# Neighbour counts made once, beside the third layer's gathers, and read back by two sum rounds

## The chip, the core and the metric

The kernel runs on one core of a Trainium2 chip. Five engines take part: PE (TensorE) for matmuls, DVE (VectorE) and ACT (ScalarE) for elementwise work, POOL (GpSimd), which here issues the gathers, and SP, whose queue carries most other transfers. The metric is the device time of one execution in microseconds; smaller is better.

## What is computed

A stack of four graph layers over 6250 nodes of 128 features, on one list of 106,250 edges sorted by target node, each followed by a residual and a layer norm:

```python
x = _layernorm(x + _L0_gnn_ref(x, edge_type_16, ...))   # two relational convolutions, 16 relations
x = _layernorm(x + _L1_gnn_ref(x, ...))                 # attention, 8 heads
x = _layernorm(x + _L2_gnn_ref(x, edge_type_8, ...))    # relational, 8 relations: the "third layer" here
x = _layernorm(x + _L3_gnn_ref(x, ...))                 # two plain mean aggregations
# in L3, twice:
msg_sum = jax.ops.segment_sum(x[src], dst, num_segments=n)
deg = jax.ops.segment_sum(jnp.ones_like(dst, dtype=x.dtype), dst, num_segments=n)
return (msg_sum / jnp.maximum(deg, 1.0)[:, None]) @ W_l.T + b + x @ W_r.T
```

The change concerns the third layer and the two sums `msg_sum` of the fourth, called sum rounds here.

## The kernel before

The edges are cut into 832 tiles of 128, and these into 104 batches of 8. A gathered batch is eight indirect DMAs issued by POOL (`gather_near`, `gather_mixed`), each of which fetches 128 rows of 512 bytes by the indices that ACT has copied into `IDX`. Matmuls with one-hot matrices made by DVE then sum the rows by target node.

**The third layer** (`near_round` with `near_c`) goes through all 104 batches, four in an iteration, with four row buffers. For batch k, PE multiplies the sums of batch k-1 by eight relation matrices (L1320, "products"), then the gathered rows by one-hots (L1330, two units of four matmuls, "near matmuls"), then places batch k-1 (L1338). ACT copies each unit out of PSUM (L942, "near copy"), copies the product (L934), and stages the indices four batches ahead (L923). DVE makes the one-hots of the next batch (L1885) and adds a placed batch to the sums (L1969).

**The sum rounds** (`mixed_round`, for `mix_a` and `mix_b`) treat every third batch without a gather: a *dense* batch. For each of its 8 tiles DVE makes two one-hots (`hot`, L2326 and L2327), PE multiplies them into counts of (source node, target) pairs (`build`, L1543), and ACT writes these to one of two blocks `NEIGH` (`take_out`, L867). PE then multiplies 49 slices of the block with the node features, split into three bf16 parts (`apply`, L1550). That makes 34 dense and 70 gathered (*sparse*) batches per round. PE's order in a step: transpose a block for the ground (L1606), half of a dense batch's products with builds for the next one between them, the ground term (L1611, L1612), and the sparse batch's eight matmuls (`collect`, L1622). POOL has four row buffers and issues batch g+3 once `collect` of g-1 is done. Every engine's order is written out by hand, and semaphores join them.

## Time and profile before

| what | us |
|---|---|
| median of 3 runs (6337.29 to 6344.32) | 6337.98 |
| profiled execution | 6346.25 |
| its span, first to last instruction | 6344.3 |
| third layer's gathered round, 3741 to 4786 | 1045 |
| first sum round, from its first gather, 4841 to 5557 | 716 |
| second sum round, 5582 to 6298 | 716 |

Over the span PE is busy for 71%, POOL for 70%, DVE for 44% and ACT for 30%. Such shares are averages over stages with different limits, so each stage has to be read by itself. An engine's busy time leaves out the instructions that only issue, load registers or wait; "idle" is told with what ended it, and "issue" is a pause in which the engine waited for nothing that the profile shows.

### The profile page before, as it was taken

The page shows a single profiled execution, that of the slowest core. Times are in us where ns is not written, and L with a number is a line of the kernel's source. Part 1 is how long each engine was busy: PE and PEld are TensorE (multiplying, and loading weights), DVE is VectorE, ACT ScalarE, POOL GpSimd, SP SyncE. Part 2 cuts the span into 40 slices and gives each one's busy share as a digit, 9 for nine tenths or more (in the row PEclk, how much of TensorE's full clock was granted, in tenths as well). Part 3 has the DMA queues.
Part 4 walks back from the last instruction along what each step waited for, and adds up shares of the span by engine and source line. Part 5 has one row for each costly group of instructions (what it writes and reads, how often), then busy time and mean ns, then how long its engine had stood idle before and what let it go on. Part 6 is the DMA issues. An engine that isn't in the chain of part 4 may idle for free. (4 is left out here: it accounts for less than half of the span.)

```text
span 6344.3 us, 119904 instructions
## 1 busy us (share of the span) xinstructions
PE 4533.7 (71%) x27080; PEld 3709.3 (58%) x27081; DVE 2761.6 (44%) x10683; ACT 1904.5 (30%) x4793; POOL 4416.5 (70%) x4559
## 2 busy tenths in 40 slices
PE   3488887878778886566666675565555888778886
PEld 3377777767777775455555555555554555555554
DVE  6643333333333332566666542222225554355543
ACT  0022222222222223444444441111114333243332
POOL 3067777757777773777777647777775777767777
PEclk6599999999999997566666688878887999989998
DMA  3066666642222211333333322111121222222222
GB/s 79 3 168 161 156 154 156 158 119 53 53 53 53 53 52 44 89 83 83 83 83 83 71 63 52 52 52 52 52 52 52 54 53 54 53 63 54 54 53 59
DMA packets 380915, 478.11 MB, mean 75 GB/s; under 512 B 123697, under 2 KB 293202, under 8 KB 380242
## 3 DMA queue, kind: packets, MB, share of 16 engines
q0 software_dynamic: 142336, 295.20, 18.3%
q1 hardware_dynamic: 233778, 174.99, 10.9%
q14 instruction: 591, 4.84, 0.2%
q10 hardware_dynamic: 4128, 1.75, 0.1%
q8 instruction: 82, 1.34, 0.1%
HBM read 447.41 MB, written 24.15 MB: 74 GB/s over the span
## 5 line engine op out<-in xcount | busy, mean ns | idle before, releaser
L1320 PE MATMUL PS<-ROOM 128*128 128x128 f32 x8320 | 1028.4, 282 | 130.6 <-ACT ROOM L942 130.6
L1320 PEld LDWEIGHTS PS<-ROOM 128*128 128x128 f32 x8320 | 972.9, 195 | 200.5 <-ACT ROOM L942 147.7
L942 ACT COPY ROOM<-PS 128x512 f32<-128x512 f32 x1040 | 609.7, 586 | 1390.5 <-PE PS L1330 1387.1
L777 POOL DMA_INDIRECT GB<-table,IDX x832 | 793.0, 953 | 316.6 <-issue 252.1
L747 POOL DMA_INDIRECT GB<-table,IDX x576 | 571.4, 992 | 217.5 <-issue 174.4
L1969 DVE TENSOR_TENSOR ROOM<-ROOM,PS 128x128 f32 x312 | 89.7, 288 | 1362.7 <-PE PS L1338 1359.0
L777 POOL DMA_INDIRECT GB<-in_x,IDX x416 | 402.8, 968 | 370.7 <-ACT IDX L923 234.0
L747 POOL DMA_INDIRECT ROOM<-table,IDX x544 | 519.1, 954 | 165.8 <-issue 164.9
L1330 PE MATMUL PS<-OH,GB 128*128 128x256 f32 (+1 forms) x1664 | 387.9, 403 | 314.4 <-DMA GB<-table,IDX 253.0
L1330 PEld LDWEIGHTS PS<-OH,GB 128*128 128x128 f32 x1664 | 326.4, 248 | 361.3 <-issue 288.2
L735 POOL DMA_INDIRECT GB<-table_gat,IDX x416 | 426.6, 1025 | 127.7 <-issue 124.2
L735 POOL DMA_INDIRECT H<-table_gat,IDX x416 | 416.6, 1002 | 126.9 <-issue 121.4
L777 POOL DMA_INDIRECT H<-in_x,IDX x416 | 404.4, 972 | 126.8 <-issue 126.8
L777 POOL DMA_INDIRECT H<-table,IDX x416 | 397.3, 955 | 126.8 <-issue 124.1
L777 POOL DMA_INDIRECT ROOM<-table,IDX x416 | 396.4, 953 | 126.8 <-issue 124.1
L1463 PE MATMUL PS<-ROOM,OH 128*128 128x144 f32 x1664 | 431.9, 453 | 1.2 <-DVE ROOM L2120 1.2
L1463 PEld LDWEIGHTS PS<-ROOM,OH 128*128 128x128 f32 x1664 | 398.2, 332 | 2.8 <-issue 1.3
L1543 PE MATMUL PS<-SPARE 128*128 128x400 bf16 x1088 | 272.6, 344 | 164.0 <-DVE SPARE L2327 144.9
L1880 DVE SCALAR_TENSOR_TENSOR H<-iota_w,key,ROOM 128x256 f32<-128x256 f32 x416 | 173.9, 482 | 345.6 <-PE PS L1330 134.5
L1330 PE MATMUL PS<-OH,ROOM 128*128 128x128 f32 x832 | 171.7, 391 | 207.7 <-DMA ROOM<-table,IDX 207.7
L1550 PE MATMUL PS<-ROOM 128*128 128x384 bf16 x1666 | 311.5, 327 | 4.5 <-issue 2.5
L1550 PE MATMUL PS<-ROOM,PACK 128*128 128x384 bf16 x1666 | 310.2, 328 | 1.7 <-issue 0.3
(386 smaller groups left out, 8405.6 us busy)
## 6 DMA issues: line engine op xcount, KB each, us to landing
H<-one_over SPq DMA_DIRECT2D x416, 128.0 KB
ROOM<-one_over SPq DMA_DIRECT2D x416, 128.0 KB
ROOM<-local_row SPq DMA_DIRECT2D x104, 256.0 KB
GB<-table,IDX POOLq DMA_INDIRECT x1408
ROOM<-table,IDX POOLq DMA_INDIRECT x960
GB<-in_x,IDX POOLq DMA_INDIRECT x416
H<-in_x,IDX POOLq DMA_INDIRECT x416
H<-table,IDX POOLq DMA_INDIRECT x416
```

The source lines that it names most:

```text
L735: pool.indirect_dma_start(out=out[:, j, :], out_offset=None, in_=r.table.dram[:, :], in_offset=bass.IndirectOffsetOnAxis(ap=idx[:, j:j + 1 ...
L747: pool.indirect_dma_start(out=RING_ROWS[c][:, j * P:(j + 1) * P], out_offset=None, in_=m.table.dram[:, :], in_offset=bass.IndirectOffsetOn ...
L777: pool.indirect_dma_start(out=r.rows[c][:, j * P:(j + 1) * P], out_offset=None, in_=r.dram[:, :], in_offset=bass.IndirectOffsetOnAxis(ap=I ...
L942: act.copy(to.rearrange("p r (j d) -> p r j d", j=r.per), of.rearrange("p (j d r) -> p r j d", j=r.per, d=NEAR))\
L1320: ins = nc.tensor.matmul(PS[:, 4, 0:P], r.near[1 - b][:, t * P:(t + 1) * P], r.weights[:, t * P:(t + 1) * P], start=t == 0, stop=t == r.re ...
L1330: ins = nc.tensor.matmul(PS[:, n, j % r.per * r.cols:(j % r.per + 1) * r.cols], r.rows[c][:, j * P:(j + 1) * P], r.hot[b][:, j * r.cols:(j ...
L1463: ins = nc.tensor.matmul(PS[:, 1 - b, 0:MW_COLS], hot(1 - b)[:, j, :], MW[:, 1 - b, j, :], start=j == 0, stop=j == G - 1)
L1543: ins = nc.tensor.matmul(PS[:, 2 * b + a, 0:KEYS // 2], HOT_LO[b], HOT_KEY[b][:, a * KEYS // 2:(a + 1) * KEYS // 2], start=True, stop=True)
L1550: ins = nc.tensor.matmul(PS[:, 4 + e, 0:3 * P], NEIGH[e][:, h, :], XS[:, h, :], start=h == 0, stop=h == XBLOCKS - 1)
L1880: ins = dve.scalar_tensor_tensor(to, columns, key, WINDOWS[b][:, j * r.cols:(j + 1) * r.cols], ALU.is_equal, ALU.mult, accum_out=wstage[:, ...
L1969: dve.tensor_tensor(dst, dst, PS[:, 5, 0:P], ALU.add).then_inc(added, 1)
```

## The change

Every four batches now form a group: the first two (16 tiles) are dense, the last two sparse. That makes 26 dense steps and 52 sparse batches per sum round. The counts of all 26 x 16 tiles are made once, in the loop of the third layer: DVE makes the one-hots (`hot_tiles`, and adds up columns in `correct`), PE multiplies them (`count_tile`) into one pair of PSUM banks, ACT takes them out (`take_out`). A tile now has 12 columns, one per node, not 16, and is written at the node's own offset in a block for 128 targets; a column that a tile shares with the one before is kept aside and added by DVE. Each finished block (`MADE_UP`, one buffer) is stored to DRAM by SP (`neighbours`); both sum rounds load blocks into the two `NEIGH` buffers. No builds are left in the sum rounds, and the one-hots of a sparse batch are one instruction, not eight. A small table (`keyed` steps) says whether a group's 16 tiles span at most 128 nodes; if not, a slow path is taken.

The core of the diff:

```diff
-KEYS = NHI * NEAR
-DENSE = BATCHES // 3
-SPARSE = BATCHES - DENSE
+SPAN = 12
+KEYS = NHI * SPAN
+PAIR = 2 * G
+CYCLE = 4
+DENSE = BATCHES // CYCLE
+SPARSE = BATCHES - 2 * DENSE
+STRIDE = 136
...
+        TILES_OF = (range(0), range(0, 5), range(5, 10), range(10, 16))
...
# SP
+            with sp.Fori(0, DENSE) as d:
+                sp.wait_ge(mx_cor, d * PAIR + PAIR)
+                sp.dma_start(neighbours[bass.ds(d, 1), :, :].rearrange("o p s -> (o p) s"), MADE_UP).then_inc(made_out, 16)
+
+            def load(m, d, e):
+                if not isinstance(d, int) or m.d0 + d >= 2:
+                    sp.wait_ge(mx_app, d + (m.d0 - 1))
+                sp.dma_start(NEIGH[e].rearrange("p h s -> p (h s)"),
+                             neighbours[bass.ds(d, 1), :, :].rearrange("o p s -> (o p) s")).then_inc(mx_ld[e], 16)
...
# ACT, third layer
+            def take_out(d, n, j, offsets):
+
+                t = d * PAIR + j
+                if j == 0:
+                    if not isinstance(d, int) or d > 0:
+                        act.wait_ge(made_out, d * 16)
+                        act.sem_inc(near_passed, 1)
+                if n == 0 and (not isinstance(t, int) or t > 0):
+                    act.wait_ge(mx_cor, t)
+                    act.sem_inc(near_passed, 1)
+                if not isinstance(t, int) or t > 0:
+                    act.wait_ge(mx_out, t)
+                    act.sem_inc(near_passed, 1)
+                act.wait_ge(mx_built, t + 1)
+                act.sem_inc(near_passed, 1)
+                if j == 0:
+                    act.copy(MADE_HALVES[:, :, :, 0:SPAN], counted_of(2)).then_inc(mx_out, 1)
+                else:
+                    act.copy(MADE_HALVES[:, :, :, bass.ds(offsets[n] + 1, SPAN - 1)], counted_of(2)[:, :, :, 1:SPAN])
+                    act.copy(SIDE[:, n, :].rearrange("p (a h) -> p a h", a=2), counted_of(2)[:, :, :, 0]).then_inc(mx_out, 1)
...
# PE, third layer
+            def count_tile(d, n, j):
+
+                t = d * PAIR + j
+                pe.wait_ge(mx_hot, t + 1)
+                if not isinstance(t, int) or t > 0:
+                    pe.wait_ge(mx_out, t)
+                for a in range(2):
+                    ins = nc.tensor.matmul(PS[:, 2 + a, 0:KEYS // 2], HOT_LO[:, n, :], HOT_KEY[n][:, a * KEYS // 2:(a + 1) * KEYS // 2],
+                                           start=True, stop=True)
+                ins.then_inc(mx_built, 1)
...
+                    tiles = TILES_OF[c] if counting and now < BATCHES else range(0)
+                    if tiles:
+                        for n in range(2):
+                            count_tile(i, n, tiles[n])
...
+                            if tiles:
+                                for at in range(2 + 2 * n, 4 if n == 0 else len(tiles)):
+                                    count_tile(i, at, tiles[at])
...
# PE, sum rounds
+                    if half == 0:
+                        pe.wait_ge(mx_ld[e], i * 16 + 16 * (m.d0 // 2 + 1))
+                        pe.sem_inc(g_passed, 1)
                     for w in range(4 * half, 4 * half + 4):
-                        if not isinstance(d, int) or d < DENSE - 1:
-                            for j in tiles_of(w):
-                                build(d + 1, j)
...
# DVE, third layer
+            def hot_tiles(d, tiles, some):
+
+                n0 = d * (CYCLE * G) + tiles[0]
+                m = len(tiles)
+                if some[0] == 0:
+                    dve.tensor_tensor(HOT_LO[:, 0:m, :], mid(iota_h[:, 0:P], m), last(lo_col[:, bass.ds(n0, m)], P), ALU.is_equal)
+                for n in some:
+                    dve.tensor_scalar(HOT_KEY[n], iota_h[:, :], near_col[:, bass.ds(n0 + n, 1)], None, ALU.is_equal).then_inc(mx_hot, 1)
+
+            def correct(d, tiles, offsets):
+
+                for n, j in enumerate(tiles):
+                    if j == 0:
+                        dve.sem_inc(mx_cor, 1)
+                        continue
+                    dve.wait_ge(mx_cor, d * PAIR + j)
+                    column = MADE_HALVES[:, :, :, bass.ds(offsets[n], 1)].rearrange("p a h o -> p (a h) o")
+                    dve.tensor_tensor(column, column, SIDE[:, n, :].unsqueeze(2), ALU.add).then_inc(mx_cor, 1)
...
+                        if mine:
+                            offsets = offsets_of(dve, i, mine)
+                            dve.wait_ge(mx_out, i * PAIR + (mine[-1] + 1))
+                            dve.sem_inc(near_passed, 1)
+                        if later:
+                            hot_tiles(i, later, range(2))
+                        if mine:
+                            correct(i, mine, offsets)
+                        if later:
+                            hot_tiles(i, later, range(2, len(later)))
...
# DVE, sum rounds
-                    for j in range(part * G // 2, (part + 1) * G // 2):
-                        ins = dve.tensor_scalar(oh(b, j), iota_f[:, :], local[:, bass.ds(n + j, 1)], None, ALU.is_equal)
-                    if part == 1:
-                        ins.then_inc(mx_oh, 1)
+                    dve.tensor_tensor(OH[:, b, :].rearrange("p (j n) -> p j n", j=G), mid(iota_f[:, :], G),
+                                      last(local[:, bass.ds(n, G)], P), ALU.is_equal).then_inc(mx_oh, 1)
```

How the order of instructions moves is seen best in three places. First ACT's own stream in the loop of the third layer, one batch of four, before:

```order
L934 COPY same<-PS 128x128
L939 ISA
L942 COPY ROOM<-PS 128x8x64
L939 REGISTER_ALU
L942 COPY ROOM<-PS 128x8x64
L923 ISA
L923 COPY IDX<-idx 128x8
```

and now, the first part of the first counted batch (`meta` is the table of offsets, `128x50x12` and `128x50x11` a tile's counts, `SPARE` the column kept aside):

```order
L997 COPY same<-PS 128x128
L586 ISA
L586 TENSOR_LOAD meta
L586 ISA x10
L967 REGISTER_ALU
L975 REGISTER_ALU
L978 CAST ROOM<-PS 128x50x12
L975 REGISTER_ALU
L980 ISA
L980 COPY ROOM<-PS 128x50x11
L981 CAST SPARE<-PS 128x50
L1007 ISA
```

Between the copy of the product and the first near copy (L1010, after the last row) there now stand a table read and two take-outs; two more follow each near copy.

Second, PE in a sum round, the second half of a dense step, before:

```order
L1606 MATMUL PS<-ident,STG 128x128
L1543 MATMUL PS<-SPARE 128x400 x2
L1550 MATMUL PS<-ROOM 128x384 x6
L1543 MATMUL PS<-SPARE 128x400 x2
L1550 MATMUL PS<-ROOM 128x384 x6
L1611 MATMUL PS<-turned,STG 128x128
L1612 MATMUL PS<-bias_rows,ones_mat 128x128
L1543 MATMUL PS<-SPARE 128x400 x2
L1550 MATMUL PS<-ROOM 128x384 x13
```

and now:

```order
L1685 MATMUL PS<-ident,STG 128x128
L1630 MATMUL PS<-ROOM 128x384 x12
L1690 MATMUL PS<-turned,STG 128x128
L1691 MATMUL PS<-bias_rows,ones_mat 128x128
L1630 MATMUL PS<-ROOM 128x384 x13
L1696 COMPARE_AND_BRANCH
L1701 MATMUL PS<-OH,GB 128x128 x8
```

The builds (L1543) that waited for DVE and ACT are gone from between the products.

Third, SP's queue after the third layer has begun, where before only the stores of the node table stood:

```order
L744 UNCONDITIONAL_BRANCH
L744 ISA
L746 ISA
L746 DMA neighbours<-ROOM 128x6800
L744 REGISTER_ALU
L744 COMPARE_AND_BRANCH
L751 DMA ROOM<-neighbours 128x6800
L751 DMA PACK<-neighbours 128x6800
L742 DMA table<-X 128x4x128 x12
```

One store per group was put into a loop, and the first two loads stand ahead of the table's stores.

## Rows read from the trace of the kernel before

**Rows 1.** Busy time by engine in three stretches; last TensorE clock, DMA share, GB/s.

```profile
3741.00:4786.00 1045.00, 607.78 (x3532) 558.89 (x3532) 226.03 (x1032) 167.32 (x425) 791.62 (x832) 0.81 0.20 52
4841.00:5557.00 716.00, 589.05 (x3676) 391.85 (x3676) 351.10 (x1351) 258.68 (x461) 545.04 (x560) 0.96 0.20 53
5582.00:6298.00 716.00, 589.45 (x3676) 392.55 (x3676) 351.51 (x1351) 258.77 (x462) 545.06 (x560) 0.96 0.20 53
```

**Rows 2.** Gathers of the sum rounds (L747): ns min/median/max; what ended POOL's idle time.

```profile
L747 POOL DMA_INDIRECT ROOM<-table,IDX x544: 941/947/1281, 4872.8 to 6277.4; - x182
...
  issue: 339.3, 1113
```

**Rows 3.** Timeline, sum round one: start, duration, engine, line, operation, idle before it.

```profile
4839.56 5.39 DVE L2542 MEMSET ROOM<- 128x6400 f32 x1 [1.28 <-ACT ROOM L842]
4841.35 0.99 POOL L747 DMA_INDIRECT GB<-table,IDX  x1 [16.80 <-DMA table<-X]
...
4849.88 11.24 POOL L747 DMA_INDIRECT GB<-table,IDX  x1 [0.30 <-issue]
...
5555.88 0.94 POOL L747 DMA_INDIRECT GB<-table,IDX  x1 [0.30 <-issue]
```

**Rows 4.** Timeline of PE inside a dense step of a sum round.

```profile
5007.57 1.14 PE L1550 MATMUL PS<-ROOM,PACK 128*128 128x384 bf16 x6
5008.55 0.50 PE L1543 MATMUL PS<-SPARE 128*128 128x400 bf16 x2
...
5010.08 1.95 PE L1622 MATMUL PS<-OH,ROOM 128*128 128x128 f32 x16
5011.87 0.39 PE L1606 MATMUL PS<-ident,STG 128*128 128x128 f32 x2
```

**Rows 5.** Two stretches: near matmuls of the third layer; a collect.

```profile
4204.80:4208.10 3.30, 3.25 (x17) 3.25 (x18) 0.00 (x0) 0.59 (x1) 2.69 (x3) 0.60 0.23 60
...
5010.00:5012.00 2.00, 2.00 (x21) 2.00 (x20) 0.82 (x3) 0.00 (x0) 1.70 (x2) 1.00 0.24 66
```

**Rows 6.** DMA issues: three loads issued together; KB, us to landing.

```profile
H<-table_gat SPq DMA_DIRECT2D x1, 1856.0 KB, 12.1
H<-table_gat SPq DMA_DIRECT2D x1, 1024.0 KB, 6.2
...
H<-table_gat SPq DMA_DIRECT2D x1, 256.0 KB, 3.0
```

**Rows 7.** Timeline of the attention round: a tensor_tensor and a gather.

```profile
2608.27 1.22 DVE L2120 TENSOR_TENSOR ROOM<-GB,ROOM 128x1024 f32<-128x1024 f32 x1
2608.57 1.73 POOL L735 DMA_INDIRECT H<-table_gat,IDX  x1 [0.30 <-issue]
```

**Rows 8.** Timeline of one batch of the third layer: PE, ACT and DVE.

```profile
4206.46 0.59 ACT L942 COPY ROOM<-PS 128x512 f32<-128x512 f32 x1 [4.91 <-PE PS L1330]
...
4208.80 2.06 PE L1320 MATMUL PS<-ROOM 128*128 128x128 f32 x16 [0.25 <-ACT ROOM L942]
4208.87 0.29 DVE L1969 TENSOR_TENSOR ROOM<-ROOM,PS 128x128 f32 x1 [6.45 <-PE PS L1338]
4210.22 1.76 DVE L1885 TENSOR_SCALAR OH<-iota_w,PACK 128x128 f32<-128x128 f32 x8 [1.06 <-DVEq L1953]
4210.90 0.27 ACT L934 COPY slots<-PS 128x128 f32<-128x128 f32 x1 [2.05 <-PE PS L1320]
...
4215.02 3.21 PE L1330 MATMUL PS<-OH,ROOM 128*128 128x128 f32 x16 [4.17 <-DMA ROOM<-table,IDX]
```

**Rows 9.** Groups of the sum round, count, busy us, mean ns: take-out, key row.

```profile
L867 ACT CAST PACK<-PS 128x800 bf16<-128x800 f32 x136 | 110.7, 828 | 140.3 <-PE PS L1543 139.2 <-issue 1.1
...
L2327 DVE TENSOR_SCALAR SPARE<-iota_h,key 128x800 bf16<-128x800 f16 x272 | 118.7, 437 | 0.0
```

**Rows 10.** Timeline at the third layer's start: DVE's first one-hots, PE's first matmuls.

```profile
3739.73 3.30 DVE L1885 TENSOR_SCALAR OH<-iota_w,PACK 128x128 f32<-128x128 f32 x16 [12.52 <-ACT ROOM L1120]
...
3752.02 3.40 PE L1330 MATMUL PS<-OH,GB 128*128 128x128 f32 x16 [13.09 <-DMA GB<-table,IDX]
```

More of the change, by code:

```diff
@@ L755, in gather_mixed @@
                         one(RING * i + c, c)
-                for g in range(RING * DOUBLES, SPARSE):
-                    one(g, g % RING)
             def gather_gat(r):
@@ L870, in step @@
-                def step(i, c, ground):
-                    e, half = c // 2, c % 2
-                    d, g = 2 * i + e, RING * i + c
-                    if ground:
+                def step(i, c):
+                    g = RING * i + c
+                    if not isinstance(g, int) or g + 3 < SPARSE:
+                        act.wait_ge(mx_sum, g * G + (m.g0 * G + TWO))
+                        stage(i + (c + 3) // RING, (c + 3) % RING)
+                    if not isinstance(g, int) or g < XBLOCKS:
@@ L895, in mixed_round @@
+                with act.Fori(1, DOUBLES - 1) as i:
                     for c in range(RING):
[L896 to L899 removed]
+                        step(i, c)
                 for c in range(RING):
[L901 to L903 removed]
+                    step(DOUBLES - 1, c)
@@ L1322, in step @@
                         ins.then_inc(made_ps, 1)
+                    tiles = TILES_OF[c] if counting and now < BATCHES else range(0)
+                    if tiles:
+                        for n in range(2):
+                            count_tile(i, n, tiles[n])
                     if now < BATCHES:
@@ L1332, in step @@
                             ins.then_inc(near_ps, 1)
+                            if tiles:
+                                for at in range(2 + 2 * n, 4 if n == 0 else len(tiles)):
+                                    count_tile(i, at, tiles[at])
                     if 1 <= now <= BATCHES:
@@ L1569, in wide @@
                             ins.then_inc(mw_p, 1)
-                        done(10 + 2 * G)
-                        for h in range(XBLOCKS):
-                            ins = nc.tensor.matmul(PS[:, 4, 0:3 * P], NEIGH[e][:, h, :], XS[:, h, :], start=h == 0, stop=h == XBLOCKS - 1)
-                        ins.then_inc(mw_p, 1)
-                        done(11 + 2 * G)
+                        done(10 + 2 * FINE)
+                        products(4, e, 0, XBLOCKS).then_inc(mw_p, 1)
+                        done(11 + 2 * FINE)
                         nc.tensor.transpose(PS[:, 5 - e, 0:P], S_SUMS[:, :], ident[:, :]).then_inc(mw_p, 1)
@@ L2308, in _ @@
             dve.wait_ge(keyed, 3)
-            dve.tensor_scalar(whole, there, 7, 4, ALU.arith_shift_right, ALU.logical_shift_left).then_inc(keyed, 1)
+            dve.tensor_scalar(whole, there, 7, None, ALU.arith_shift_right).then_inc(keyed, 1)
             dve.wait_ge(keyed, 4)
@@ L2467, in step @@
                     first = isinstance(d, int) and d == 0
-                    more = not isinstance(d, int) or d < DENSE - 1
-                    before = (i, c - 1) if c > 0 else (i - 1, RING - 1)
-                    if half == 0:
-                        if more:
-                            hot(d + 1, 0)
-                            hot(d + 1, 1)
-                        if not first:
-                            reduce(d - 1, 1 - e)
-                            put(i, 1 - e, d - 1)
-                    elif more:
-                        hot(d + 1, 5)
+                    if half == 0 and not first:
+                        reduce(d - 1, 1 - e)
+                        put(i, 1 - e, d - 1)
                     if not (first and half == 0):
-                        k = batch_of(*before)
+                        k = batch_of(i, c - 1) if c > 0 else batch_of(i - 1, RING - 1)
                         flag, base = meta_of(dve, k, 0, 2)
```

419 lines of the change are left out of this document (220 added, 199 removed).

## The prediction

> **What bounds the kernel now.** I first read the stretches [rows 1], to learn how long each stage lasts and who is busy in it. The change touches three: the third layer's gathered round (1045 us, 104 batches) and the two plain sum rounds (716 us each). In none of them is TensorE the limit by its busy time: 608 of 1045 us, 589 of 716. GpSimd counts as busy for only 545 of 716 us, so the second view must say what ends its idle time [rows 2]: over both sum rounds 339.3 us of it, in 1113 pieces, is "issue", that is the 0.30 us between two gathers in which nothing is waited for; so it never waits long for a buffer or an index. A gather itself lasts 0.947 at the median. So one gather costs 0.947 + 0.305 = 1.252 us, and a sum round is 560 of them in a row. The timeline confirms it [rows 3]: the first starts at 4841.35, the last at 5555.88 and ends 715.5 us after the first began. 560 x 1.252 = 701.1; one gather of 11.24 us, which should have taken 0.95, is 10.3 of the rest, and some 4 us are small delays. The third layer's round has the same pace: 832 x 1.252 = 1041.7 of its 1045 us, or 40.06 us for four batches. A stage with fewer gathers is shorter until something else in it takes longer.
>
> **What the change removes.** Each sum round gathers 52 batches, not 70: 416 gathers, 144 fewer. At 1.252 us that is 180.3 us per round. The 26 dense steps left cover 16 tiles each with the same 49 products that covered 8. On TensorE six products start to finish in 0.98 us (5007.57 to 5008.55), 0.163 each; a collect of eight takes 1.79 us (5010.08 to 5011.87); a single fp32 matmul as in the ground 0.39 at most [rows 4], and I give the three of the ground 1.0 together. The 34 x 16 builds and their ACT copies leave these rounds. A dense step with its two collects, two grounds and its placing (0.3) is then 49 x 0.163 + 2 x 1.79 + 2 x 1.0 + 0.3 = 13.9 us, against 20.0 us for GpSimd's 16 gathers: GpSimd still bounds the round. TensorE would have to run at under 0.7 of its clock to change that; after some 4 us of idleness it was granted 0.60 over 3.3 us, near its lower level of 1.2 GHz, and back to back 1.00, the level of 2.4 GHz [rows 5], so I keep that for the range.
>
> **What it adds to the sum rounds.** Two things.
> First, each dense step loads its counts, 128 x 13,600 bytes = 1700 KB, on SP's queue once the products two steps earlier are done, a whole dense step (21 us) and more before they are wanted. The nearest transfers are three loads issued together, 3136 KB in all, of which the last landed after 12.1 us [rows 6]: 259 KB/us. A load is at least 6.6 us plus about 2 to start, 8.6, and about 10.5 if the gathers' 53 GB/s [rows 1] run beside it. It is covered by the step between; it costs something only beyond 24 us.
> Second, the one-hot rows of a sparse batch, eight tensor_scalar before, become one tensor_tensor of 1024 elements with both inputs in SBUF. The trace of before has that shape in the attention round: 1.22 us, and the gather that began 0.30 us after it took 1.73 us instead of 0.947 [rows 7]. So a gather that starts while it runs waits for its end, less about 0.14 us (0.92 us were left, 0.78 were lost). The cost per batch lies between 0, when it falls between two gathers' starts, and 1.1 us; for a start at a random moment it is 1.08 x 1.08 / 2 / 1.252 = 0.47 us. Times 52: 24 us per round, bounds 0 and 57. The 11.24 us gather fits the same cause, since VectorE splits the rows at that moment and still will; I keep 10.3 + 3.
> The Trainium skill (SBUF — State Buffer, section Who interferes with whom) says that a VectorE instruction with two SBUF inputs contends only with a GpSimd instruction that reads SBUF, and infers that writing descriptors is not held up by it. By that inference the term would be 0 and the sum 48 us lower; the 1.73 us row speaks against it, perhaps because the gather reads its indices from SBUF.
> A sum round: 416 x 1.252 + 10.3 + 3 + 24 = 558, so 157 less than 715.5, and **313 us less for both** (249 to 363).
>
> **What it adds to the third layer.** In three of every four batches 5, 5 and 6 tiles are counted: two matmuls into PSUM banks 2 and 3, of which there is one set; ACT copies 550 elements into the block and 50 beside it; the next count waits for that copy. I add up one step from the end of its eight weight products, at full clock, with these durations: products 2.06, a near copy 0.59, ACT's copy of 128 elements 0.27, VectorE's add 0.29, a read of one table value with its branch 1.06 [rows 8]; 800 elements out of PSUM 0.83 on ACT, a key row of 800 on VectorE 0.44 [rows 9]. From 0.83 and 0.59 (512 elements) an element is 0.84 ns: a take-out is 0.62 for 550 and 0.20 for 50, 0.82 us. A count of 600 columns is put at 0.35, under the 0.50 of a build of 800 [rows 4]. A read of several offsets is not in the trace; I take 1.1, near its only row.
> ACT's small copy, the read and the first take-out end at 2.2. The second count 2.6, four near matmuls (half of 1.79) 3.5, the near copy 4.15, the third take-out 4.95 (the second ran beside the matmuls), the fourth count 5.3, matmuls 6.25, near copy 6.9; the fifth count and the placing fit beside it. Products again: **9.2 us**. The second counted step has a second read: 10.3. The third has a sixth tile, which waits for the fifth's take-out (+1.5), and its first take-out waits for VectorE's corrections of the step before, about 5.1 us after the placing (add 0.3, two reads 2.2, the low rows 0.9, two keys 0.7, five corrections 1.0) where ACT is ready after 3.7: 12.1. The step without counting: 4.9. Sum 36.5.
> Then the block itself: there is one, and the next group's first take-out waits until it is stored. The store starts some 2.6 us after the third step's placing and lands 8.6 to 10.5 us later, at about 12.1; the take-out is otherwise ready at 2.3 + 4.9 + 1.4 = 8.6. ACT stalls 3.5 us, and behind it stand the near copies, for which TensorE waits. That makes 40.0, just GpSimd's 40.06. But about ten hand-overs in the chain carry nothing for semaphore waits and address registers; rows 8 show 0.04 us (products end 4210.86, ACT 4210.90) to 0.25 between dependent engines, and I take 0.3 each because every take-out waits for registers too: **43.0 us** per four batches. The indices for the gathers are copied by ACT four batches ahead, so GpSimd is held only by the average, not by a single stall. 26 x (43.0 - 40.06) = **76 us more**. Bounds: GpSimd keeps the pace and loses only to the low rows' tensor_tensor (two of 640 and one of 768 elements, 0.55 us per four batches by the price above), +14; and 49 us, if matmuls run at 0.60 and the reads cost twice as much, +232.
>
> **At no cost.** Some twenty small table instructions, a memset and two tiny transfers come before the third layer. VectorE was idle there for 12.5 us, and the first near matmul starts 12.3 us after the first hot row [rows 10]. I estimate 11 us of instructions (the 6400-element memset in rows 3 took 5.4) and 5 of transfers, which end some 4 us into that second gap. Without that cover it would be 4 us, once. A pair of batches that spans over 128 nodes would take a slow path; the first nodes of the reference's own edges give 116 to 125.
>
> **The sum.** -313 + 76 = -237 us. It is made against the profiled execution: 6346 becomes 6109. The median of the runs, 6338, is 8 us lower, so I predict **6101 us**.
>
> **Rivals.**
> 1. GpSimd still bounds the third layer (hand-overs nearly free, a store under 8 us): 6338 - 313 + 14 = **6039**. For it: the chain without hand-overs comes to 40.0. Chance 0.24.
> 2. The counting chain takes four batches past **52.1 us** and the kernel is **slower**: 26 x (52.1 - 40.06) = 313 is the point where all is given back. If nothing overlaps, 16 tiles at 0.35 + 0.82 + two hand-overs of 0.3 are 28, four bare steps 21, four reads 4.4 and the store's stall 4.6: 58 us, +466, **6491**. Against it: TensorE, ACT and VectorE have 4 to 7 us of idleness per batch in rows 8, and near matmuls stand between the counts. Chance 0.09.
> 3. The sum rounds do not get their full gain: the tensor_tensor always hits (57 us per round) or the loads or a low clock hold TensorE; with the first alone 6101 + 66 = **6167**. Chance 0.10.
> 4. The tensor_tensor never holds a gather up in the sum rounds: 6101 - 48 = **6053**. The 1.73 us row is against it: chance 0.05. (It is what the inference of the Trainium skill's SBUF — State Buffer, Who interferes with whom, would give.)
> 5. The slow path is taken after all: hundreds of us more; 0.01.
>
> **How the numbers follow.** My forecast, a chain of 41.5 to 47 us, has 0.51: 6062 to 6205. Rivals 1, 3 and 4 lie between 6000 and 6235, so 6000 to 6235 holds about 0.8; above it are chains of 48 us and more, below it a round without any lock. What can be told from no change is 0.2%, 13 us. Faster 0.88, same 0.02, slower 0.10.
>
> **What would show it.** In the profile after: 416 gathers per sum round, idle before them "issue", 545 to 591 us from first to last; gathers of 1.1 to 2 us where the 1024-element tensor_tensor runs. Loads landing in 8 to 12 us and no wait of TensorE for them. In the third layer POOL's idle time should now name ACT's index copy, some 3 us per four batches, and ACT should wait for the store at every first take-out. If POOL's idle there stays "issue", rival 1 is right; if the round passes 1300 us, rival 2. If gathers in the sum rounds wait for ACT or the collects for TensorE, the first part of the sum is wrong.

## The result and the profile after

The changed kernel is slower by 0.6%: **6371.87 us** (median of six runs, 6365.82 to 6395.28) against 6337.82 of the kernel before (six runs, 6337.29 to 6344.32), a ratio of **1.0058**, 95% interval 1.0042 to 1.0074. The profiled execution took 6382.97 us, its span 6381.1. Forecast were 6101 us and a range of 6000 to 6235.

The stretches of the profile after, with the columns of [rows 1]: the third layer's gathered round, what follows it up to the first gather of the sum rounds, and the two sum rounds.

```profile
3742.00:5126.50 1384.50, 800.22 (x4265) 650.10 (x4266) 539.40 (x1868) 462.39 (x1194) 806.49 (x832) 0.73 0.23 71
5126.50:5218.70 92.20, 39.88 (x234) 34.47 (x234) 53.06 (x132) 36.78 (x158) 10.74 (x14) 0.70 0.30 99
5218.70:5762.60 543.90, 407.40 (x2434) 294.26 (x2434) 137.80 (x257) 43.74 (x171) 417.37 (x416) 0.88 0.41 131
5790.40:6334.60 544.20, 401.59 (x2434) 291.82 (x2434) 136.58 (x256) 43.47 (x172) 417.67 (x416) 0.88 0.40 128
```

The sum rounds gave 172 us each, 344 together. The third layer took 1384.5 us instead of 1045, and 92 us instead of 55 lie between its last gather and the first of the sum rounds: from first gather to first gather 1476 us for 1100, 376 us more. The granted clock of the third layer fell from 0.81 to 0.73. 376 - 344 = 32 us more; the medians differ by 34.

The gathers of the sum rounds by source line, as in [rows 2]:

```profile
L811 POOL DMA_INDIRECT GB<-table,IDX x416: 938/945/1957, 5218.7 to 6312.9; - x139
...
  issue: 251.1, 824
...
  ACT IDX L919: 1.8, 6
```

GpSimd still bounds them: its idle time is the 0.30 us between two gathers. In the third layer it no longer does. The waits of four engines there (engine, line, what was waited for, us in total, times, longest):

```profile
POOL ROOM L839 <- ACT IDX L986: 252.2, 49, 7.5
PE PS L1346 <- ACT SPARE L981: 278.4, 189, 3.6
PE PS L1346 <- DVE PACK L1944: 193.9, 74, 5.4
ACT ROOM L980 <- DVE ROOM L1954: 197.4, 50, 5.4
ACT slots L997 <- PE PS L1404: 161.9, 50, 4.4
DVE OH L1974 <- DVEq L2042: 131.4, 53, 4.8
DVE PACK L1942 <- issue: 129.4, 50, 3.0
DVE ROOM L1954 <- issue: 81.9, 25, 3.5
```

GpSimd waits for ACT's copies of indices, ACT for the corrections (L1954), TensorE's counts (L1346) for ACT's take-outs (L980, L981) and for key rows (L1944), and VectorE, apart from the placing matmul (L1429), for no other engine by these rows: "issue" before the low rows (L1942) and the corrections is the read of the tiles' offsets into registers (e8_no_reads, which leaves the read out, leaves next to nothing there), and DVEq before the near rows (L1974) is its own sequencer. The third counted step of one cycle, the loop's end behind it, the block's store and the first count of the next cycle:

```profile
4333.30 0.29 DVE L2058 TENSOR_TENSOR ROOM<-ROOM,PS 128x128 f32 x1 [4.22 <-PE PS L1429]
4334.08 2.02 PE L1404 MATMUL PS<-ROOM 128*128 128x128 f32 x16 [1.10 <-PEq L1396]
4336.14 0.27 ACT L997 COPY same<-PS 128x128 f32<-128x128 f32 x1 [2.24 <-PE PS L1404]
4336.60 0.96 DVE L1942 TENSOR_TENSOR PACK<-iota_h,etype 128x768 bf16<-128x768 f16 x1 [3.01 <-issue]
4337.90 0.43 PE L1346 MATMUL PS<-PACK 128*128 128x300 bf16 x2 [1.80 <-DVE PACK L1944]
4338.04 2.46 DVE L1954 TENSOR_TENSOR ROOM<-ROOM,SPARE 128x50 bf16 x5
4340.92 0.68 ACT L980 CAST ROOM<-PS 128x550 f32 x1 [4.52 <-DVE ROOM L1954]
4341.83 0.66 PE L1346 MATMUL PS<-PACK 128*128 128x300 bf16 x2 [3.50 <-ACT SPARE L981]
4342.28 1.91 PE L1418 MATMUL PS<-OH,ROOM 128*128 128x128 f32 x8
...
4351.21 0.29 DVE L2058 TENSOR_TENSOR ROOM<-ROOM,PS 128x128 f32 x1 [7.06 <-PE PS L1429]
4351.92 3.78 PE L1404 MATMUL PS<-ROOM 128*128 128x128 f32 x16 [1.03 <-PEq L1396]
4354.77 3.02 DVE L1954 TENSOR_TENSOR ROOM<-ROOM,SPARE 128x50 bf16 x6 [3.27 <-issue]
4357.95 0.33 SPq L746 DMA_DIRECT2D neighbours<-ROOM  x1
...
4366.13 0.68 PE L1346 MATMUL PS<-PACK 128*128 128x300 bf16 x2 [5.07 <-DVE PACK L1944]
```

TensorE's products end at 4336.10, and it is ready for the step's first count; ACT still has its own read of offsets ahead of the first take-out (e2_side shows it). But VectorE reads offsets until 4336.60, for 3.0 us, so that the key row is there at 4337.9; then come five corrections, 0.49 us each in the mean; only behind them may ACT take out the first count (4340.92), since it would overwrite the side sums that the corrections read. The second count starts 5.7 us after the products' end. By then TensorE runs at the lower clock: four near products take 1.91 us, a count 0.66 to 0.71. The next cycle's first count waits 5.1 us for its key row, which VectorE makes only behind these corrections, the loop's end, the near rows and an add.

### The profile page after: what moved, and what is told of

Its sections match the earlier page's. It is cut to its first block and busy times, and to the rows that moved or that the text cites. A ratio compares the mean times of both kernels' runs of the same rounds, so it can differ in the third digit from the quotient of the medians.

```text
span 6381.1 us, 116473 instructions
## 1 busy us (share of the span) xinstructions
PE 4386.8 (69%) x25432; PEld 3624.8 (57%) x25433; DVE 2671.0 (42%) x9398; ACT 1784.3 (28%) x5020; POOL 4172.8 (65%) x4271
## 3 DMA queue, kind: packets, MB, share of 16 engines
q0 software_dynamic: 133120, 276.30, 16.9%
## 5 line engine op out<-in xcount | busy, mean ns | idle before, releaser
L1404 PE MATMUL PS<-ROOM 128*128 128x128 f32 x8320 | 1058.4, 287 | 171.9 <-ACT ROOM L1010 103.5
L1404 PEld LDWEIGHTS PS<-ROOM 128*128 128x128 f32 x8320 | 999.2, 199 | 237.4 <-ACT ROOM L1010 124.1
L839 POOL DMA_INDIRECT GB<-table,IDX x832 | 801.1, 963 | 393.6 <-issue 245.9
L1010 ACT COPY ROOM<-PS 128x512 f32<-128x512 f32 x1040 | 609.9, 586 | 890.5 <-PE PS L1418 890.1
L839 POOL DMA_INDIRECT ROOM<-table,IDX x416 | 402.7, 968 | 376.4 <-ACT IDX L986 252.2
L811 POOL DMA_INDIRECT GB<-table,IDX x416 | 417.0, 1002 | 170.9 <-issue 125.2
L1346 PE MATMUL PS<-PACK 128*128 128x300 bf16 x624 | 186.8, 396 | 479.3 <-ACT SPARE L981 253.7
L811 POOL DMA_INDIRECT ROOM<-table,IDX x416 | 418.1, 1005 | 126.8 <-issue 125.9
L1346 PEld LDWEIGHTS PS<-PACK 128*128 128x128 bf16 x624 | 53.2, 113 | 568.4 <-DVE SPARE L1944 216.3
L980 ACT CAST ROOM<-PS 128x550 f32 x390 | 259.2, 665 | 390.6 <-DVE ROOM L1954 204.2
L1418 PE MATMUL PS<-OH,H 128*128 128x256 f32 x832 | 226.8, 434 | 95.6 <-DMA H<-in_x,IDX 53.9
```

The source lines that it names most:

```text
L811: pool.indirect_dma_start(out=RING_ROWS[c][:, j * P:(j + 1) * P], out_offset=None, in_=m.table.dram[:, :], in_offset=bass.IndirectOffsetOn ...
L839: pool.indirect_dma_start(out=r.rows[c][:, j * P:(j + 1) * P], out_offset=None, in_=r.dram[:, :], in_offset=bass.IndirectOffsetOnAxis(ap=I ...
L980: act.copy(MADE_HALVES[:, :, :, bass.ds(offsets[n] + 1, SPAN - 1)], counted_of(2)[:, :, :, 1:SPAN])
L1010: act.copy(to.rearrange("p r (j d) -> p r j d", j=r.per), of.rearrange("p (j d r) -> p r j d", j=r.per, d=NEAR))\
L1346: ins = nc.tensor.matmul(PS[:, 2 + a, 0:KEYS // 2], HOT_LO[:, n, :], HOT_KEY[n][:, a * KEYS // 2:(a + 1) * KEYS // 2], start=True, stop=True)
L1404: ins = nc.tensor.matmul(PS[:, 4, 0:P], r.near[1 - b][:, t * P:(t + 1) * P], r.weights[:, t * P:(t + 1) * P], start=t == 0, stop=t == r.re ...
```

## The experiments

In the table the counted steps are c1 (tiles 0 to 4), c2 (5 to 9) and c3 (10 to 15), c0 is the batch without counting; each is the mean, over 16 to 22 cycles of the trace, from one start of ACT's copy of the weight products (L997) to the next. "Third layer" goes from its first gather to the first of the sum rounds. Kernels ran on several chips, on which the kernel before took 6336 to 6348 us; the third column is free of that. Of the changed kernels only the kernel after, e15_scalars and e16_warm_all ran more than once; where two kernels share the third layer, its time agrees within 2.3 us (1476.4 and 1476.1 in the kernel after and e7_scalars; 1174.3, 1172.0 and 1174.0 in e12_all, e15_scalars and e16_warm_all).

| kernel | time, us | third layer | c0 | c1 | c2 | c3 | cycle |
|---|---|---|---|---|---|---|---|
| before | 6337.8 | 1100 | | | | | 40.1 (GpSimd) |
| forecast | 6101 | 1176 | 4.9 | 9.2 | 10.3 | 12.1 | 36.5; 43.0 with store and hand-overs |
| after | 6371.9 | 1476 | 5.3 | 16.0 | 13.7 | 19.8 | 54.8 |
| e1_no_count | 5995.8 | 1097 | | | | | |
| e2_side | 6324.1 | 1415 | 5.0 | 16.9 | 13.4 | 17.3 | 52.6 |
| e8_no_reads | 6304.7 | 1408 | 5.1 | 16.8 | 13.5 | 17.1 | 52.5 |
| e9_act | 6212.8 | 1316 | 5.4 | 16.6 | 11.0 | 15.7 | 48.6 |
| e10_next | 6365.0 | 1476 | 5.2 | 15.1 | 14.2 | 20.1 | 54.6 |
| e11_keys | 6108.6 | 1203 | 5.2 | 17.6 | 9.6 | 12.0 | 44.4 |
| e12_all | 6069.0 | 1174 | 4.7 | 16.2 | 9.6 | 12.5 | 43.0 |
| e13_warm | 6304.8 | 1412 | 5.0 | 17.4 | 12.6 | 17.3 | 52.3 |
| e14_first | 6081.7 | 1192 | 5.8 | 15.7 | 9.6 | 12.8 | 43.9 |

**e1_no_count.** The counting is switched off on three engines; the store waits for the batches instead.

```diff
-sp.wait_ge(mx_cor, d * PAIR + PAIR)
+sp.wait_ge(added, d * FOUR + (2 * BATCHES + FOUR))
-near_round(near_c, PARTS_C, residual, True)
+near_round(near_c, PARTS_C, residual, False)
... (the same on ACT and VectorE)
```

> The counting is left out of the third layer; what is stored is the cleared block, one store for every four batches as before, and the sum rounds load those blocks, so that their sums are wrong. Time from the third layer's first gather to the first gather of the sum rounds: 1100 us in the kernel before, 1478 in the changed one. Theory (the counting chain holds TensorE, ACT and VectorE up, and nothing else in the change does): back to 1100 to 1115, the sum rounds stay at about 545 each, total 5995. Rival (the stores of 1700 KB on SP's queue or their contention with the gathers take a share of the loss): above 1150, total above 6040.

Measured: 5995.8 us; the two stretches from the third layer to the sum rounds, and the first sum round:

```profile
3730.30:4772.40 1042.10, 603.08 (x3532) 555.15 (x3532) 228.94 (x1035) 167.03 (x425) 788.77 (x832) 0.80 0.29 94
4772.40:4827.50 55.10, 20.09 (x134) 19.36 (x134) 37.24 (x79) 21.83 (x121) 10.34 (x14) 0.69 0.46 155
4827.50:5370.90 543.40, 400.42 (x2434) 290.21 (x2434) 138.23 (x258) 43.63 (x171) 416.94 (x416) 0.89 0.39 131
```

The total is within 1 us of the theory's: the stores (94 GB/s in the stretch for 71 in the kernel after) cost the gathers nothing. All 376 us are the counting chain, the 37 us behind the last gather too. (With the counting ACT's wait for the store is gone as well; what that wait costs is seen in e10_next.)

**e2_side.** Side sums in 16 places, ACT's wait for the corrections taken out with its cause.

```diff
-if n == 0 and (not isinstance(t, int) or t > 0):
-    act.wait_ge(mx_cor, t)
-act.copy(SIDE[:, n, :]...)
+act.copy(SIDE[:, j, :]...)
... (the same index in `correct`)
```

> The 50 side sums of each tile get a place of their own (16 places instead of 6), so that ACT's first take-out of a step no longer waits for VectorE's corrections of the step before. Theory A (this wait is on the path): the first take-outs of the second and third counted step of a cycle start 2.0 and 2.5 us after their count instead of 0.2, so up to 26 x 4.2 = 109 us come back: 6263. Rival B (the late key rows of VectorE are on the path, the corrections only stand beside them): the third count, whose key row comes behind the corrections, takes the place of the wait, less than 30 us come back: above 6340.

Measured: 62 us less in the third layer, between the two. Only c3 fell, by 2.5 us. The timeline shows what stood behind the wait:

```profile
4299.86 0.43 PE L1343 MATMUL PS<-PACK 128*128 128x300 bf16 x2 [0.87 <-DVE PACK L1941]
...
4302.02 0.68 ACT L977 CAST ROOM<-PS 128x550 f32 x1 [2.73 <-issue]
```

The count is done at 4300.29, and ACT, with nothing to wait for, begins 1.7 us later: it too reads the offsets, 2.7 us for five values in two loads.

**e8_no_reads.** The corrections go to a fixed column, and VectorE reads no offsets.

```diff
-offsets = offsets_of(dve, i, mine)
+offsets = [0] * len(mine)
-column = MADE_HALVES[:, :, :, bass.ds(offsets[n], 1)]...
+column = MADE_HALVES[:, :, :, 0:1]...
```

> VectorE's reads of the tiles' offsets are left out; the corrections all go to column 0, so that the counts at the tiles' borders are wrong. VectorE is idle 2.2, 3.0 and 3.3 us before the work that follows these reads in the three counted steps; the prediction had 1.1, 2.2 and 2.2. Theory B (late key rows): the low rows start 1.9 and 2.7 us earlier in the second and third step and the corrections of the third step 3 us earlier, which lets the key rows of the next cycle come earlier; 26 x 5 to 7.5 us come back: 6180 to 6240. Rival A (the wait for the corrections alone counts, and it shrinks only with the corrections' start): 26 x 4.6, about 6250, with ACT still waiting 2 to 2.5 us for VectorE at those take-outs. Rival C (reads lie beside TensorE's work): nothing, 6365 to 6380.

Measured: 69 us less, far under theory B and under rival A, though not nothing. ACT's own read now stands where the corrections stood, as in e2_side. And at the loop's end nothing came back:

```profile
4311.75 0.29 DVE L2058 TENSOR_TENSOR ROOM<-ROOM,PS 128x128 f32 x1 [7.29 <-PE PS L1429]
4312.06 2.46 DVE L1954 TENSOR_TENSOR ROOM<-ROOM,SPARE 128x50 bf16<-128x50 bf16 x6
4322.87 1.80 DVE L1974 TENSOR_SCALAR OH<-iota_w,PACK 128x128 f32<-128x128 f32 x8 [8.35 <-issue]
```

From the add to the next cycle's first near row pass 11.1 us; in the kernel after 11.3 (4351.21 to 4362.47, this line):

```profile
4362.47 1.67 DVE L1974 TENSOR_SCALAR OH<-iota_w,PACK 128x128 f32<-128x128 f32 x8 [4.68 <-DVEq L2042]
```

What VectorE saves ahead of the loop's end it waits there. The trace shows where in the kernel after: the branch at the loop's end (L2089) and the sequencer's next instruction (times executed, duration in ns, start in us), first in the kernel after, then in e1_no_count:

```profile
L2089 DVEq COMPARE_BRANCH  x1: 63/63/63, 4357.5 to 4357.5; - x1
L2089 DVEq FUSED_REGOPS  x1: 85/85/85, 4360.4 to 4360.4; - x1
```

```profile
L2089 DVEq COMPARE_BRANCH  x1: 63/63/63, 4216.7 to 4216.7; - x1
L2089 DVEq FUSED_REGOPS  x1: 85/85/85, 4217.1 to 4217.1; - x1
```

With the counting 2.9 us lie from the branch to the next instruction, without it 0.3 to 0.4; the near rows come 4.7 us after the last correction, and in e1_no_count 1.6 at most after the add. In e8_no_reads the same branch takes 2.8 us, and a second one, past the slow path (L2040), some 4 more, from 4318.7 to 4322.6. That fits a loop that has outgrown what the engine keeps of its program: the queue that brings instructions moved 650 packets in the kernel after and 518 in e1_no_count, five per cycle more. But the kernel before moved 591 and has the short branch, and no experiment took this apart, so it stays a reading. The Trainium skill (Runtime: NRT & Kernel Launch, section Instruction fetch mechanics) states the rule that would make it so: a taken branch whose target is not in the window held must wait until it is fetched. The 2.9 and 4 us behind taken branches agree with it; what the engine waited for there is not in the trace.

**e9_act.** As e2_side, and ACT reads its offsets before it waits for the products.

```diff
+if tiles:
+    offsets = offsets_of(act, i, tiles)
 if 1 <= now <= BATCHES:
     act.wait_ge(made_ps, K)
...
-    offsets = offsets_of(act, i, tiles)
```

> Side sums with a place of their own as in e2_side, and ACT reads the offsets of its tiles at the head of its step, before it waits for the eight weight products, and no longer behind its copy of them. In the trace of e2_side ACT's first take-out with an offset still begins 2.7 to 2.9 us after its count, and nothing is waited for: the read of four or five table values. Theory D (ACT's read took the place of the wait that e2_side removed): the second and third counted step fall by 2.0 to 2.5 us each, 26 x 4.5 = 117 us from e2_side's 6324: 6207. Rival B (then the late key row of the third count takes its place): under 40 us, above 6285.

Measured: 99 us less than e2_side in the third layer, c2 and c3 down by 2.4 and 1.6: theory D, with 99 of its 117 us. In e9_act it is still TensorE's products that end ACT's idle time before its copy of them, so the read is free there. This is the pattern of the whole case: the corrections and ACT's read lay over each other, and either alone explained the late take-out.

**e10_next.** The keys of the next cycle's c1 at the end of c3.

```diff
+if c == FOUR - 1 and now < BATCHES - FOUR:
+    dve.wait_ge(mx_built, i * PAIR + (mine[-1] + 1))
+    hot_tiles(i + 1, TILES_OF[1], range(len(TILES_OF[1])))
... (and none behind the loop's end)
```

> One edit against the changed kernel: the low and key rows of a cycle's first counted step are made at the end of the cycle before (beside the last counts' take-outs, ahead of the corrections) and not behind the loop's end. Theory (TensorE's wait of 4.7 to 5.4 us for the first key row, after VectorE's corrections and 4.6 us at the loop's end, is on the path): the first counted step falls from 16.0 to about 11.5 us, and the corrections come 2.6 us later, which nobody waits for in that step: 26 x 4.5 = 117 us less than 6372: 6255. Rival (VectorE is merely late there and would hold up the same batch with its near rows, whose first is made 4.6 us after the loop's end too): under 40 us, above 6330.

Measured: nothing (1476 us), as the rival said, but not for its reason. c1 fell by only 0.9 us:

```profile
4347.21 0.42 PE L1346 MATMUL PS<-PACK 128*128 128x300 bf16 x2
...
4351.90 0.66 ACT L978 CAST ROOM<-PS 128x600 bf16<-128x600 f32 x1 [4.22 <-DMA neighbours<-ROOM]
...
4352.70 0.66 PE L1346 MATMUL PS<-PACK 128*128 128x300 bf16 x2 [5.07 <-ACT ROOM L978]
```

The count is early, and now ACT waits 4.2 us for the block's store, which the late key row had covered. The store is the stall that the prediction had; c2 and c3 took back the rest (14.2 and 20.1).

**e11_keys.** As e9_act, and VectorE makes the next step's keys before it reads offsets and corrects.

```diff
-offsets = offsets_of(dve, i, mine)
-dve.wait_ge(mx_out, i * PAIR + (mine[-1] + 1))
+dve.wait_ge(mx_built, i * PAIR + (mine[-1] + 1))
-hot_tiles(i, later, range(2))
+hot_tiles(i, later, range(len(later)))
+offsets = offsets_of(dve, i, mine)
+dve.wait_ge(mx_out, i * PAIR + (mine[-1] + 1))
```

> As e9_act, and VectorE makes the key rows of the next counted step as soon as TensorE has done the last count of this one, ahead of its read of the offsets and of the corrections. Theory B: the first count of the second and third counted step, which waits 0.9 to 1.8 us for its key row, starts at once, and with ACT's wait gone as well the two steps fall to 11 to 12 us and 13 us; 26 x 1.5 to 2.5 less than e9_act: 40 to 65 us. Rival (take-outs one after the other from one pair of banks, 5 x 1.7 us at the low clock, set the step by now): within 20 us of e9_act.

Measured: 113 us less than e9_act, twice what theory B gave. c2 and c3 are at 9.6 and 12.0. More came back than the key's lateness. The clock between 3850 and 4750 us is 0.85, for 0.82 in e9_act and 0.73 in the kernel after, which can be a part of it; the rest was not taken apart.

**e12_all.** e11_keys with the keys of e10_next.

```diff
+if c == FOUR - 1:
+    if now < BATCHES - FOUR:
+        hot_tiles(i + 1, TILES_OF[1], range(len(TILES_OF[1])))
... (else the next step's, as in e11_keys)
```

> As e11_keys, with the key rows of a cycle's first counted step made at the end of the cycle before, as in e10_next. Theory: the edits add up, since each takes a wait from a different step: 6372 - 48 (e2_side) - 117 - 50 - 117 = 6040, a cycle of 40 to 42 us, and GpSimd's 40.06 us per four batches comes into sight (with it as the only bound 5996, as without counting). Rival (the take-outs' own chain at the low clock holds the cycle at 45 us and more): 6125 or above.

Measured: 6069.0 us, between the two; a cycle of 43.0 us. The third layer, and its waits for the store between 3850 and 4800 us:

```profile
3730.20:4821.00 1090.80, 652.99 (x4266) 536.78 (x4266) 556.70 (x1870) 460.72 (x1194) 803.99 (x832) 0.88 0.28 90
```

```profile
ACT ROOM L975 <- DMA neighbours<-ROOM: 118.8, 22, 6.6
```

The edits do not add up, they unlock each other: 62 us for the side places alone, 1 for the early keys alone (29 behind the other three), and 302 with ACT's read and the order of the keys, which were not tried alone; VectorE still reads its offsets, only where nobody waits. By the trace what is left in c1 is the store, 5.4 us per cycle, and the loop's end; no run takes either away.

**e13_warm.** Useless matmuls while TensorE waits for the first take-out; nothing else is changed.

```diff
+for _ in range(10 if n == 0 else 0):
+    nc.tensor.matmul(PS[:, 6, 0:2 * P], ident[:, :].bitcast(BF16)[:, 0:P], ident[:, :].bitcast(BF16), start=True, stop=True)
```

> The changed kernel with ten more matmuls of 256 bf16 columns behind the first count of every counted step, into a bank that nobody reads: work without use for TensorE in the 2.9 to 3.8 us in which it waits for the first take-out. In the third layer the granted clock is 0.73, and the four near products between the counts take 1.92 us where they take 1.05 at full clock, a count 0.66 to 0.71 instead of 0.43. Theory E (the lower clock is a part of the loss): clock above 0.85, near products 1.05 and counts 0.43 in the second half of each counted step, where they stand in the chain; 4 to 8 us per cycle come back, 26 x 4 to 8 = 105 to 210 us: 6165 to 6265. Rival (VectorE and ACT set the steps, TensorE only waits less or more): within 40 us of 6372, or slower if the added matmuls (1.1 us at full clock, 2.1 at half) stand in the way.

Measured: 6304.8 us, 65 us less in the third layer, and under the kernel before. The stretch from 3850 to 4750 us in the kernel after and in this one:

```profile
3850.00:4750.00 900.00, 523.40 (x2787) 424.62 (x2788) 350.32 (x1210) 304.15 (x784) 511.92 (x528) 0.73 0.23 72
```

```profile
3850.00:4750.00 900.00, 527.00 (x3436) 426.24 (x3437) 366.76 (x1274) 318.13 (x825) 542.39 (x553) 0.88 0.23 74
```

The clock rose as theory E said, c3 and c2 fell by 2.5 and 1.1, but c1 rose by 1.4, where the added matmuls ran at the lower clock and stood before the second count. So part of the loss is the clock, which fell because of the waits: 65 us of the 376, net of what the added matmuls cost, where theory E had 105 to 210.

**e14_first.** In c3 the corrections before the next keys.

```diff
 correct(i, mine, offsets)
+if c == FOUR - 1 and now < BATCHES - FOUR:
+    hot_tiles(i + 1, TILES_OF[1], range(len(TILES_OF[1])))
```

> As e12_all, but in the last counted step of a cycle VectorE makes the corrections first and the next cycle's five key rows behind them, so that the block's store starts about 2.5 us earlier. In e12_all ACT waits 5.4 us for that store in every cycle at the first take-out, and TensorE behind it. Theory F (with the other waits gone the store is on the path): 26 x 2 to 2.5 = 50 to 65 us less than e12_all, 6005 to 6020. Rival (the key and near rows, then late by the loop's end of some 5 us, take its place): within 25 us of 6069.

Measured: 17 us more than e12_all in the third layer, the rival. The store went earlier, c1 fell by 0.5, c0 and c3 rose by 1.4 together; VectorE's keys stand before the loop's end, with its branch, and there are 5.2 us of sequencer behind them:

```profile
4318.37 1.94 DVE L1972 TENSOR_SCALAR OH<-iota_w,PACK 128x128 f32<-128x128 f32 x8 [5.17 <-DVEq L2040]
```

**e7_scalars.** Eight tensor_scalar for the sparse one-hot rows of the sum rounds again.

```diff
-dve.tensor_tensor(OH[:, b, :]..., mid(iota_f[:, :], G), last(local[:, bass.ds(n, G)], P), ALU.is_equal)...
+for j in range(G):
+    ins = dve.tensor_scalar(oh(b, j), iota_f[:, :], local[:, bass.ds(n + j, 1)], None, ALU.is_equal)
+ins.then_inc(mx_oh, 1)
```

> The one-hot rows of a sparse batch in the sum rounds are made by eight tensor_scalar again, as before the change. The prediction gave the one tensor_tensor 24 us of held-up gathers per sum round (0 to 57). If that is right, a sum round takes 545 - 24 = 521 us and the total is 48 us lower, 6324. Rival (a tensor_tensor of this shape holds no gather up): 545 us as now, 6372. Rival (eight instructions cost more in waits of the tables' columns): longer than 545.

Measured: 6334.8 us, the sum rounds 522.0 and 521.2:

```profile
5212.00:5734.00 522.00, 403.58 (x2434) 291.66 (x2434) 161.59 (x622) 43.67 (x171) 395.53 (x416) 0.90 0.41 137
```

```profile
L811 POOL DMA_INDIRECT GB<-table,IDX x416: 940/944/1267, 5211.9 to 6263.7; - x139
```

22 us per round, where the prediction had put 24: the one tensor_tensor holds the gathers up. In the three kernels with eight tensor_scalar a sum round takes 521.0 to 522.0 us, in the ten with the one tensor_tensor 538 to 546, so 16 to 25 us by kernel. VectorE's busy time is longer (162 for 138 us) and the round shorter. The longest gather falls from 1957 to 1267 ns. One that was held up, in the kernel after:

```profile
5320.87 1.22 DVE L2458 TENSOR_TENSOR OH<-iota_w,local 128x1024 f32<-128x1024 f32 x1 [0.54 <-issue]
5321.11 1.79 POOL L811 DMA_INDIRECT GB<-table,IDX  x1 [0.30 <-issue]
```

**e15_scalars and e16_warm_all**, four runs each: all gains together, and with twenty useless matmuls behind the first count of a cycle.

```diff
+for _ in range(20 if j == 0 else 0):
+    nc.tensor.matmul(PS[:, 6, 0:2 * P], ident[:, :].bitcast(BF16)[:, 0:P], ident[:, :].bitcast(BF16), start=True, stop=True)
```

> e12_all together with e7_scalars: the edits of the third layer and of the sum rounds lie in different stages, so their gains should add up: 6069 - 37 = 6032 (6020 to 6045), 0.951 to 0.954 of the kernel before. If it is above 6055, the two are not independent.

> e15_scalars with twenty useless matmuls of 256 bf16 columns behind the first count of each cycle, where TensorE waits 5.7 us for ACT and ACT for the block's store. Theory E (clock): behind that wait two counts take 0.66 to 0.71 us and four near products 1.92 us in e12_all, where full clock gives 0.43 and 1.05, so 1 to 1.5 us per cycle come back: 26 to 39 us, 5993 to 6006. Rival (VectorE's near rows, made 5 us after the loop's end, hold that step anyway): within 10 us of e15_scalars.

Measured: e15_scalars **6025.3 us, ratio to the kernel before 0.9514 (0.9498 to 0.9530)**, as expected: the two stages are independent. e16_warm_all 6027.8, 0.9516 (0.9500 to 0.9531): no gain, the rival. The clock did come, as the lines behind the wait show, and c1 fell by 0.8 to 15.4, but c0 and c3 took 0.7 back:

```profile
4310.57 0.42 PE L1344 MATMUL PS<-PACK 128*128 128x300 bf16 x2 [2.06 <-ACT ROOM L975]
4310.83 1.10 PE L1418 MATMUL PS<-OH,GB 128*128 128x128 f32 x8
```

## Why the prediction was wrong

**What bounds the kernel, and the sum rounds: right, with the gain a little too small.** 558 us were forecast per round, 544 measured. Of the terms, 416 x 1.252 = 521 holds by itself (e7_scalars: 522.0 and 521.2), the tensor_tensor is 22 where 24 was put, and the 13 for one long gather and small delays did not come: the longest gather is 1.96 us, where [rows 3] have one of 11.24; why that one is gone was not looked into. The loads of 1700 KB were covered: no product of TensorE waits for one, and but for 32 us before its first product its long waits in the round are for gathers.

**The third layer: the step that failed.** +76 us were forecast, +376 came. The failing step is "I add up one step from the end of its eight weight products": one thread of work was followed through a step, with VectorE's key rows taken as ready at its start, and ACT's and VectorE's table reads as 1.1 us each. Between 4 and 7 us of idleness per batch [rows 8] were taken for room. It was room at the wrong moment: in this kernel's order VectorE's reads, keys and corrections start only when a step's counts are over, which is just when the next step needs them. In the third step alone the sum had this chain, with 5.1 us from the placing to the corrections' end, and the lines above have 7.2 (4333.30 to 4340.50). e11_keys and e12_all, which take these from the path, bring c2 and c3 to 9.6 and 12.0 to 12.5 us, where the sum had 10.3 and 12.1, and the third layer to 1174 us, where the sum had 1176. So c2 and c3 were added up well for a kernel in which keys and offsets come early; this one makes them late. That the whole meets the sum is partly luck: in e12_all c1 takes 16.2 us, where the sum with the store's stall had 12.7, the hand-overs put on top were too long, and c3 no longer has the wait for corrections that its 12.1 holds.

**The sizes within it.** Offsets: 2.2 us for one read of five values, 3.0 for five in two reads and 3.3 for six in one on VectorE, 2.7 to 2.9 on ACT, where 1.1 per read was put: the row nearest to it [rows 8] had one value. Most of it is not the load but the register instructions behind it, one set for each value; for the five values of one first counted step in the kernel after (the engine's sequencer; ns min/median/max):

```profile
L586 DVEq FUSED_REGOPS  x6: 81/183/190, 4319.9 to 4321.7; - x6
L586 DVEq TENSOR_LOAD <-meta x1: 600/600/600, 4320.0 to 4320.0; - x1
```

A correction: 0.49 us, where 0.2 was put. Four near products 1.91 and a count 0.66 to 0.71 after a wait, where full clock was put (0.9 and 0.35); the range had 0.60 of the clock only together with the slow reads. A take-out 0.87 (0.66 and 0.20), where 0.82 was put. The ten hand-overs of 0.3 are too high: 0.15 to 0.2 stand between count and take-out in the timelines. The loop's end of 4.7 us, 1.6 at most before, was not in the sum at all.

**The store: near in size, by luck, and wrong in place.** A stall of 3.5 us per cycle was forecast. The store was to start 2.6 us after the placing and starts 6.7 after it (4351.2 to 4357.95), behind the slow read and the corrections; it lands sooner, which nearly makes up for that. In the kernel after ACT waits for the store once, since the late key row of c1 covers it (it lands in 6.3 us at the median, where 8.6 to 10.5 were put); in e10_next and e12_all, without that cover, it is 4 to 6.6 us a cycle.

**The tail: missed.** ACT copies the indices four batches ahead, so the gathers run ahead of the counting. The prediction took this as a reason why a single stall costs nothing; it also means that some three batches of the slow chain are left when the last gather is done. VectorE's last add is at 5173.91, 47 us after it, and at 4796.68 in the kernel before, 10 us after: 37 us.

**The rivals.** Rival 2 was the case: its point was 52.1 us per four batches, 1384.5 / 26 = 53.2 came, past its sign of 1300 us for the round, and it had 0.09. Its price, 6491 for no overlap at all, was too high. Its "against" was the idleness in [rows 8] again. Rival 4, that the tensor_tensor holds no gather up, is refuted by e7_scalars: 22 us per round, gathers of 1.00 us in the mean against 0.95. The inference in the Trainium skill (SBUF — State Buffer, section Who interferes with whom) would give that rival; these runs speak against it. The slow path was not taken.

## What to carry to other kernels

When work is put beside a tuned loop, idle time of the engines is no measure of room: ask of each added instruction when its input is there and when its output is wanted, and add the wait up across steps, from the last reader of a buffer to the next writer. Where a step is late, look for several waits that lie over each other, and take them away together before judging any; alone two of them gave 62 us and 1 us here, four together 302. Read table values into registers at a moment when the engine waits anyway, and make the next step's operands before the clean-up of this one.

## What the runs showed of the hardware

- A read of five or six table values holds an engine up for 2.2 to 3.3 us. In the read of 2.2 us the load itself takes 0.60, and the register instructions behind it, with what lies between them, some 0.27 for each value. The Trainium skill (Runtime: NRT & Kernel Launch, section Instruction fetch mechanics) has about 200 ns per register for such a load, by which five would take an estimated 1.0; here the table lies in SBUF, and the load of five took 0.60, so that the larger part is what stands behind the load.
- A tensor_tensor of 1024 elements with both inputs in SBUF lengthens the gather that starts while it runs, from 0.94 to as much as 1.96 us in the kernel after; eight tensor_scalar of 128 elements in its place leave no gather above 1.27.
- Five tensor_tensor of 50 elements at addresses from registers, each waiting for the one before, take 2.46 us; at a fixed address (e8_no_reads) six take the same 2.46.
- Useless matmuls made the third layer 65 us faster (e13_warm): the granted clock of the stretch went from 0.73 to 0.88, and four near products behind the first take-out of c2 and c3 from 1.92 to 1.10 us.
- In every kernel with the counting 2.7 us or more pass on VectorE between the loop's branch and its next instruction (in e14_first 4.8 and more), 0.3 in the kernel before and in e1_no_count; the cause was not taken apart.
